# Second softmax of a graph attention layer: 23 of 79 source columns looked up by gathers on GpSimd

## The reference

```python
as_n = jnp.einsum('nhd,hd->nh', h, a_src)
ad_n = jnp.einsum('nhd,hd->nh', h, a_dst)
e = jax.nn.leaky_relu(as_n[src] + ad_n[dst], NEG_SLOPE)
e_max = jax.lax.stop_gradient(jax.ops.segment_max(e, dst, num_segments=N))
ex = jnp.exp(e - e_max[dst])
denom = jax.ops.segment_sum(ex, dst, num_segments=N)
alpha = ex / (denom[dst] + 1e-16)
```

## Time and profile before

| | |
|---|---|
| Median of three runs | 4167.94 us (4165.6 to 4171.07) |
| Profiled execution | 4167.93 us |
| Its span (first to last instruction) | 4166.2 us |
| Mean granted clock of TensorE | 0.939 |
| PE, DVE, ACT, POOL busy over the span | 86%, 53%, 33%, 20% |
| Second softmax, from the barrier before it to the one after | 3484.4 to 3594.4 us |

### The profile page before, as it was taken

How to read it: one execution, slowest core, us unless ns; L and a number is a source line. 1 busy time by engine, 2 the same in 40 slices (tenths; PEclk the granted TensorE clock), 3 DMA queues, 4 the chain that set the end, 5 groups by cost and what they waited for, 6 DMA issues and landing times. The chain is left out here.

```text
span 4166.2 us, 68773 instructions
## 1 busy us (share of the span) xinstructions
PE 3571.3 (86%) x22440; PEld 2183.9 (52%) x22441; DVE 2228.8 (53%) x5433; ACT 1354.7 (33%) x2327; POOL 850.1 (20%) x1236
## 2 busy tenths in 40 slices
PE   4860019999999999999999999999999996388888
PEld 3640015565556556655655565566556654256565
DVE  8877345334434443443344344434443434699998
ACT  2531104323322332333233223323332333244444
POOL 2448720000000000100000000000000100266665
PEclk9985559999999999999999999999999998699999
DMA  8862011111111111111111111121111100378887
GB/s 256 256 213 83 3 27 41 55 40 46 39 58 36 45 42 54 41 39 48 39 51 38 55 37 43 42 60 36 42 45 40 53 27 15 84 207 231 233 236 209
DMA packets 142471, 337.79 MB, mean 81 GB/s; under 512 B 76839, under 2 KB 76917, under 8 KB 134775
## 3 DMA queue, kind: packets, MB, share of 16 engines
q1 hardware_dynamic: 111976, 240.96, 19.0%
q0 software_dynamic: 29056, 92.87, 8.6%
q10 hardware_dynamic: 1175, 0.05, 0.0%
HBM read 266.01 MB, written 124.25 MB: 94 GB/s over the span
## 5 line engine op out<-in xcount | busy, mean ns | idle before, releaser
L1394 PE MATMUL lay_pm<-lay_zh,w1h 128*128 128x500 f16 x1920 | 718.9, 374 | 26.0 <-DVE lay_h L1280 19.6
L1117 POOL DMA_INDIRECT lay_rows<-parts,lay_idx x200 | 209.7, 1048 | 2536.7 <-PE lay_pz L1360 1616.3
L1395 PE MATMUL lay_pm<-lay_zl,w1h 128*128 128x500 f16 x1920 | 719.2, 375 | 3.2 <-issue 3.1
L1396 PE MATMUL lay_pm<-lay_zh,w1l 128*128 128x500 f16 x1920 | 718.9, 374 | 0.0
L1201 DVE SCALAR_TENSOR_TENSOR lay_zl<-lay_pz,lay_zh 128x400 f16<-128x400 f32 x600 | 319.5, 573 | 708.3 <-ACT lay_zh L1311 708.3
L1311 ACT ACTIVATE lay_zh<-lay_pz 128x400 f16<-128x400 f32 x600 | 297.9, 503 | 1054.2 <-PE lay_pz L1360 1050.2
L1320 ACT ACTIVATE lay_ex<-lay_pm,b1c,scale 128x500 f32<-128x500 f32 x320 | 245.5, 767 | 873.7 <-PE lay_pm L1396 873.7
L1418 PE MATMUL lay_pm<-w2h,lay_gh 128*128 128x512 f16 x1280 | 485.0, 379 | 0.0
L1418 PE MATMUL lay_pm<-w2h,lay_gl 128*128 128x512 f16 x1280 | 483.9, 378 | 0.0
L1418 PE MATMUL lay_pm<-w2l,lay_gh 128*128 128x512 f16 x1280 | 483.4, 378 | 0.0
L1236 DVE TENSOR_SCALAR lay_ex<-lay_ex,scale 128x500 f32<-128x500 f32 x320 | 153.6, 480 | 571.8 <-ACT lay_ex L1320 571.8
(11 more groups left out here) (308 smaller groups left out, 5600.6 us busy)
## 6 DMA issues: line engine op xcount, KB each, us to landing
x<-in_x_dram SPq DMA_DIRECT2D x20, 1500.0 KB
out_x<-x SPq DMA_DIRECT2D x100, 288.0 KB
out_own<-h SPq DMA_DIRECT2D x100, 288.0 KB
out_dram<-out_x SPq DMA_DIRECT2D x100, 288.0 KB
nrm_xb<-in_x_dram SPq DMA_DIRECT2D x20, 1344.0 KB
parts<-nrm_parts SPq DMA_DIRECT2D x20, 1344.0 KB
h<-lay_h SPq DMA_DIRECT2D x80, 336.0 KB
nrm_w<-in_L_gnn_W_dram SPq DMA_DIRECT2D x6, 1024.0 KB, 19.6
```

Source lines behind the costliest of these rows:

```text
L1394: pe.matmul(o, c.w1h[:, d, cols], zh[:, d, h], start=(d == 0), stop=False)
L1395: pe.matmul(o, c.w1h[:, d, cols], zl[:, d, h], start=False, stop=False)
L1396: ins = pe.matmul(o, c.w1l[:, d, cols], zh[:, d, h], start=False, stop=(d == DC - 1))
```

## The change

Of the sources' 79 columns, only the first 56 are looked up by `Match`; the last 23 are gathered by GpSimd from the same table in HBM, with the code that the first softmax uses. The destinations' columns are all matched as before. VectorE waits for the 23 gathers after the last sum of `Match` and before the first use of the looked-up values (L856).

```diff
     SIDES = (("src", 1, 4), ("dst", 2, 3))
+    GATHERED = 23
 ...
         self.items = [(side, at, min(group, EC - at)) for side, (_, _, group) in enumerate(self.SIDES)
-                      for at in range(0, EC, group)]
+                      for at in range(0, EC, group) if side or at < EC - self.GATHERED]
 ...
             if match:
                 match.gpsimd(pool)
-                return
             pool.wait_ge(loaded, 16 * 9)
-            for idx, out, sem in ((src, gsrc, got_src), (dst, gdst, got_dst)):
-                for k in range(EC):
+            for idx, out, sem in ((src, gsrc, got_src), (dst, gdst, got_dst))[0:1 if match else 2]:
+                for k in range(EC - match.GATHERED if match else 0, EC):
                     nc.gpsimd.indirect_dma_start(out[:, k, :], None, table[:, :], bass.IndirectOffsetOnAxis(
                         ap=idx[:, k:k + 1], axis=0), bounds_check=N - 1, oob_is_err=False).then_inc(sem, 16)
 ...
             if match:
                 match.vector(dve, ch)
+                dve.wait_ge(got_src, 16 * match.GATHERED)
             else:
```

## The result

| | before | after |
|---|---|---|
| median of six runs, us | 4167.55 (4163.74 to 4171.07) | 4184.33 (4181.48 to 4186.53) |
| ratio with its 95% interval | | 1.0040 (1.0027 to 1.0053) |
| profiled execution, us | 4167.93 | 4181.48 |
| its span, us | 4166.2 | 4179.7 |
| first memset of the stage to the reader of the logits, us | 84.54 | 98.92 |

The kernel is 0.40% slower. The spans differ by 13.5 us: the stage starts 0.5 us later, takes 14.4 us longer up to its reader, and what lies behind the reader takes 1.3 us less (597.07 and 595.74 us). So the loss lies inside the second softmax. In the changed kernel the lines of the matching class and of what follows it are numbered one higher: the picks are L682, the sums L672, the products L735, the spreads L743, ScalarE's two steps L710 and L703; the gathers are L819.

A forecast was written before the change was run, and what follows sets the result against it. VectorE was taken to bound the second softmax's matching loop. Removed groups -8.19, head +0.2 and added wait +0.05 give -7.94 us, so 4167.93 becomes 4160.0 us, range 4155 to 4166.

The forecast's parts named there:

- What bounds the kernel, and what is removed: Second softmax's matching: VectorE bounds the loop; dropping source groups 14 to 19 removes 8.27 less 0.08, 8.19 us.
- When the gathers run, and the cover: Gathers start near 3490.5, 1.30 us apart, last at 3519.1, landed near 3521.7; reader at 3560.9, 39 us of cover.
- the added wait: VectorE's wait for 23 gathers before the first sum of logits: already met, 0 to 0.11 us, taken as 0.05.
- longest seen: Longest gathers in the first softmax, 2.89 us beside a large SBUF comparison; cover gone at 3.09 us start to start.
- What they do to VectorE in the head: Before the first picks, three gathers meet small SBUF-to-SBUF instructions: 0.2 us added, bounds 0 and 3.0 us.
- What they do to picks and sums: Beside VectorE's picks and sums in the match, gathers were taken to cost nothing.
- longer picks and late gathers: Signs of a wrong prediction: picks over 0.92 us for four beside gathers, or last gather starting much after 3519.
- Cost zero: The 23 gathers themselves, landing 39 us ahead of their reader in the second softmax, add no time.
- The witness: First softmax's rows, which gave gather times and VectorE reductions of 2210 to 2212 ns with gathers beside all.
- picks and sums are held: Rival: all 23 gathers hold VectorE in the match for 1.00 us each, giving 4182.8 us; chance 0.06.
- The stage behind: Output stage starts 8 us earlier with the same work: zero taken, 3 us each side; as a rival, chance 0.15.

The follow-up runs named there:

- cut_only: The changed kernel without its 23 gathers, those columns filled with zeros by one GpSimd instruction; ratio 0.9987, stage 76.40 us.
- all_matched_plus_23: The kernel before, all 79 columns matched, with 23 gathers beside the match into a tensor nobody reads; ratio 1.0052, stage 106.69 us.
- plus_23_wide: The kernel before with 23 back-to-back gathers of 32-byte rows (first layer's logits) into a tensor nobody reads; ratio 0.9998, stage 84.59 us.
- first_sum: The changed kernel with its 23 gathers back to back, but begun only behind the first sum; ratio 1.0045, stage 102.70 us.

## Why the prediction was wrong, point by point

- **What bounds the kernel, and what is removed: right.** VectorE's chain sets the sources' time, and six groups fewer gave 8.14 us (cut_only) of 8.19.
- **When the gathers run, and the cover: right.** First gather 3491.05 (forecast 3490.5, the stage began 0.5 us later), 1.30 us apart, last 3519.68, 64 us ahead of the reader. The reader starts at 3584.00 without idle time before it, so the added wait was met. The "longest seen" of 2.89 us overlooks the 3117 ns in the earlier trace rows, which is over the 3.09 us at which the cover ends; here no gather took more than 1.02 us, so that did no harm.
- **What they do to VectorE in the head: the cost of 0.2 us was too high here.** Four gathers start in the head, not three, as 3490.5 + 3 x 1.30 = 3494.4 already says. The small instructions beside the first gather last 0.19 to 0.21 us (in all_matched_plus_23 two of them 0.43 and 0.36). Of the 2.7 us by which the first picks are late, 2.5 are the late increment of the first products (3498.58 to 3501.09).
- **What they do to picks and sums: right, and of no help.** 0.92 and 0.47 us, unstretched. The prediction had named longer picks and late gathers as what would prove it wrong; there were neither, and the kernel was slower all the same.
- **"Cost zero" for the gathers themselves: this step failed.** It priced a gather by what it does to VectorE and by its own landing. It had no term for TensorE's increments, on which both VectorE and ScalarE start each group. They cost 22.5 us: 2.7 in the head and 19.8 in the sources. The witness was also a poor one. Hardly a handoff of TensorE lies beside the gathers of the earlier trace rows, as its timeline in the first softmax of the kernel before shows (below), so they couldn't have shown the harm. They also carry rows of 32 bytes, those of the change 8; whether that matters is open, since plus_23_wide is from a chip on which nothing stalled.
```profile
336.23 0.82 PE L493 MATMUL sm_pw<-sm_before,ones 128*1 128x200 f32 x2 [46.80 <-DVE sm_row L514]
355.93 0.37 PE L496 MATMUL sm_pm<-ident,sm_top 128*4 128x128 f32 x1 [18.88 <-DVE sm_diag L536]
```

- **The rival "picks and sums are held"** gave 4182.8 us, and 4184.3 came, but by the wrong mechanism: 23 holds of 1.0 us each on VectorE don't exist. It would have advised other instructions on VectorE, which would have changed nothing.
- **The stage behind** gave 1.3 us back, inside the 3 us allowed.

Shown by these runs: the loss is TensorE's increments coming late beside gathers that follow each other at 1.30 us (cut_only, all_matched_plus_23, and the table of increments), and eleven gathers 5.6 us and more apart do no such harm on a chip on which eleven at 1.30 us do. Not the reason, since the stall comes without them: the table, destinations that stand close together, rows of exactly 8 bytes, a start before the first product, a low clock, the shorter loop.

Not shown, since each rests only on runs from chips 10 and 5: that 1.41 or 1.70 us is far enough, that rows of 32 bytes are harmless, that the destinations' groups are (they differ from the sources' in length, 1.62 for 1.41 us, in their spreads, in the size of the picks, and in that TensorE runs 296 matmuls in 43.09 us of them and 319 in 28.12 us of the sources), and that SyncE's small DMAs are.

Open as well: what inside the chip the increments and the gathers share. The recording itself is a rival. Each time on record comes with a span and a granted clock, so all of these executions were recorded; wherever TensorE's increments were late by more than 1 us, 64 to 78% of the gathers' landings in this stage are missing from the record, and where there was no stall, at most 31 of 368 are. No execution without recording was timed, so no run tells whether the stall would be there then.

## What to carry to other kernels

Take the price of an operation from a place in which the handoffs that you depend on lie beside it: gathers of 1.00 us each show no harm in the first softmax, where TensorE hands over hardly anything, and cost 22 us in the second. Look at handoffs, not only at durations: set the end of a product beside the start of the instruction that waits for it, above all where the profile names a releaser that makes no sense. When gathers run beside a loop that lives on short handoffs, try tying one gather to each turn of the loop: the kernels with that one wait stood at 0.9976 and 0.9980, and at 0.9966 with more columns, though on other chips than the changed kernel with its 1.0040. And run the kernel that shows the effect again beside every kernel that is to be free of it, on the same chip. Eight runs here lack that partner, and it costs them their meaning as explanations.

## What the runs showed of the hardware that was not expected

- TensorE's increments were up to 18.6 us late in the changed kernel and up to 21.3 us in first_sum, beside back-to-back gathers of 8-byte rows, where those of VectorE and ScalarE that are on record came within 0.02 us; 0.01 us is the usual distance for TensorE as well.
- With 1.30 or 1.31 us from gather to gather beside the sources they were held in all nine runs that had it with rows of 8 or 16 bytes, on four numbered chips and on that of the changed kernel. With 5.6 us and more on one of these chips they were not held by more than 0.26 us.
- A gather of 128 rows takes 1.00 us on GpSimd and 1.30 from start to start, with rows of 8, 16 and 32 bytes alike.
- Memsets of 512 columns in GpSimd's stream of gathers went with small instructions of VectorE of up to 0.76 us for 0.19, and with a head 1.95 us longer; gathers alone stretched two of them, to 0.43 and 0.36 us, in one kernel of seven.
- The traces of the first softmax, the same code in all runs, hold 1736 to 2337 of 2528 landing increments on some chips and 2527 or 2528 on others.
